# Expert results of a routed layer: six picked rows a token, or two token-ordered sums in DRAM built by adding writes

## The reference

```
scores = sigmoid(xf @ w_router)                      # 1024 tokens, 32 experts
topk_idx = 6 experts of each token, out of 4 groups  # chosen by scores + corr_bias
topk_w = scores at topk_idx
y[token] = sum over its 6 experts e of
    topk_w * ( (silu(h @ gate_w[e]) * (h @ up_w[e])) @ down_w[e] )
y = y + shared expert(h)                             # dense, width 352
x = x + gb * y                                       # gb per sequence and channel
```

## Time and profile before

| | us |
|---|---|
| timed runs, median of 3 (lowest to highest) | 442.95 (440.52 to 444.48) |
| span of the profiled execution, first to last instruction | 442.4 |
| expert stage, first to last tile_hidden (L1800) | 112.2 to 251.7 |
| products of the shared expert for sequence 1 (L664) begin | 256.1 |
| first product of layer 1 (L843 on x_r) begins | 283.6 |
| PE busy / DVE busy / ACT busy / POOL busy | 409.2 / 293.6 / 207.5 / 129.4 |

### The profile page before, as it was taken

The page is one execution under the profiler, slowest core; times in us unless marked ns, Lnnn a source line. Parts: engine busy times, 40 slices in busy tenths (PEclk is TensorE's granted clock), DMA queues, the critical chain, the costliest instruction groups (busy, mean ns, idle before and its releaser), DMA issues. The chain is left out here.

```text
span 442.4 us, 6194 instructions
## 1 busy us (share of the span) xinstructions
PE 409.2 (93%) x1923; PEld 305.7 (69%) x1924; DVE 293.6 (66%) x710; ACT 207.5 (47%) x390; POOL 129.4 (29%) x143
## 2 busy tenths in 40 slices
PE   6996888888999999999998899899999979999997
PEld 6453737445677777777776636787677858798886
DVE  4899986898444444444444465989786998886542
ACT  2598935473222222222222237482796487722430
POOL 1000011003777777777777500601000010010000
PEclk9989788997999999999999969999999998999999
DMA  7986665890333233333239249911500000000001
GB/s 272 418 377 150 150 154 142 305 425 26 100 103 107 98 104 107 95 101 106 101 101 276 74 162 369 331 74 28 185 1 0 1 1 1 1 1 35 12 1 48
DMA packets 24010, 56.89 MB, mean 129 GB/s; under 512 B 4528, under 2 KB 15794, under 8 KB 22996
## 3 DMA queue, kind: packets, MB, share of 16 engines
q1 hardware_dynamic: 18564, 41.80, 28.0%
q0 software_dynamic: 5424, 14.82, 10.2%
HBM read 46.10 MB, written 10.50 MB: 128 GB/s over the span
## 5 line engine op out<-in xcount | busy, mean ns | idle before, releaser
L732 PE MATMUL bank<-arena,tile_mem 128*128 x224 | 75.6, 460 | 0.0
L1406 POOL DMA_INDIRECT tile_mem<-h_dram,gidx x57 | 56.1, 984 | 52.5 <-DVE gidx L1784 35.5
L1394 POOL TENSOR_TENSOR rstd<-ve,mhalf 128x2 f32<-128x2 f32 (+1 forms) x14 | 11.2, 800 | 192.1 <-DVE ve L1533 192.1
L1413 POOL DMA_INDIRECT y_dram<-norm,didx x56 | 55.4, 990 | 22.7 <-issue 13.7
L1800 DVE TENSOR_TENSOR tile_mem<-tile_mem,bank 128x176 f32<-128x176 f32 x56 | 18.9, 338 | 62.3 <-ACT tile_mem L1204 62.3
L748 PE MATMUL bank<-arena,tile_mem 88*128 x224 | 57.9, 380 | 0.8 <-DVE tile_mem L1795 0.8
L748 PEld LDWEIGHTS bank<-arena,tile_mem 88*128 88x128 f32 x224 | 42.4, 189 | 15.8 <-issue 1.0
L843 PE MATMUL bank<-x_r,f_r 128*128 128x512 f32 x192 | 46.6, 403 | 0.8 <-DVE x_r L1980 0.7
L732 PEld LDWEIGHTS bank<-arena,tile_mem 128*128 128x128 f32 x224 | 38.2, 190 | 11.8
L1204 ACT ACTIVATE tile_mem<-bank 128x176 f32<-128x176 f32 x56 | 17.8, 317 | 57.4 <-PE bank L732 57.4
L843 PEld LDWEIGHTS bank<-x_r,f_r 128*128 128x128 f32 x192 | 36.9, 194 | 10.0 <-issue 0.8
(11 more groups left out here) (290 smaller groups left out, 740.7 us busy)
## 6 DMA issues: line engine op xcount, KB each, us to landing
arena<-w_gu SPq DMA_DIRECT2D x3, 2112.0 KB, 12.3
arena<-w_dn SPq DMA_DIRECT2D x4, 1408.0 KB
arena<-w_gu SPq DMA_DIRECT2D x2, 2464.0 KB, 21.1
arena<-y_dram SPq DMA_DIRECT2D x6, 768.0 KB, 9.0
arena<-w_f SPq DMA_DIRECT2D x6, 512.0 KB, 6.9
arena<-wmod SPq DMA_DIRECT2D x3, 512.0 KB, 9.1
arena<-wmod SPq DMA_DIRECT2D x2, 768.0 KB, 10.7
arena<-y_dram SPq DMA_DIRECT2D x4, 384.0 KB, 5.5
```

The lines of the kernel that those rows point to most:

```text
L732: mm = pe.matmul(bank[2 + r % 2][:, 0:2 * M], xgT[r % 2][:, k * P:(k + 1) * P], gu[:, bass.ds(e[k], 2 * M)], start=(k == 0), stop=(k == CT ...
L1406: pool.indirect_dma_start(out=xg[j % 4], out_offset=None, in_=h2_dram, in_offset=bass.IndirectOffsetOnAxis(ap=gidx[:, j:j + 1].bitcast(U32 ...
L1413: pool.indirect_dma_start(out=y_dram, out_offset=bass.IndirectOffsetOnAxis(ap=didx[:, j:j + 1].bitcast(U32), axis=0), in_=yt[j % 4], in_of ...
```

## The change

The experts' results are no longer stored apart and picked up later. Two tensors in DRAM, `sum_dram[0]` and `sum_dram[1]`, have one row a token and 128 rows for empty slots. They start with zeros (and, in the first, with the shared expert's result for sequence 0), and the scatter of tile j adds its 128 rows into the one of number j % 2. The score is multiplied in before: it is gathered together with the token's row, since `h2_dram` now has 32 more columns that hold `scores`, and `tile_hidden` multiplies by the column of the tile's expert, whose number DVE reads from `eoff` once a quad. After the experts, SP loads two rows a token in place of six.

With it go other waits: a gather waits for `tile_hidden` of tile j-4 (it used to wait for `tx`); `copy_y` of tile j waits until the scatter of tile j-2 has landed (it used to be j-4); LAG goes from 6 to 5; the sums of sequence 0 are made by DVE alone, behind `shared_hidden`.

```diff
-LAG = 6
+LAG = 5
...
-    h2_dram = nc.dram_tensor("h2_dram", (B * S, C), F32, kind="Internal").ap()
+    h2_dram = nc.dram_tensor("h2_dram", (B * S, C + E), F32, kind="Internal").ap()
-    y_dram = nc.dram_tensor("y_dram", ((TOPK + 1) * B * S, C), F32, kind="Internal").ap()
+    sum_dram = [nc.dram_tensor(f"sum_dram{i}", (P + B * S, C), F32, kind="Internal").ap() for i in range(2)]
...
@@ SP @@
+            sp_.wait_ge(zeros_ready, 1)
+            for i, blocks in ((0, (0, 1)), (0, (1 + TB, 1 + NT)), (1, (0, 1 + NT))):
+                n = blocks[1] - blocks[0]
+                rows = sum_dram[i].rearrange("(n p) c -> p n c", p=P)[:, blocks[0]:blocks[1], :]
+                sp_.dma_start(rows, zeros.unsqueeze(1).to_broadcast([P, n, C])).then_inc(sums_start, 16)
             sp_.wait_ge(modT_done, 2)
             for e in range(0, DN_LATE, 8):
                 sp_.dma_start(dn[:, e * DNW:(e + 8) * DNW], w_dn[:, e * DNW:(e + 8) * DNW]).then_inc(dn_in, 16)
...
-                sp_.dma_start(h2v[:, b * TB:(b + 1) * TB, :], norm[:, b * TB:(b + 1) * TB, :]).then_inc(h2_out, 16)
+                sp_.dma_start(h2v[:, b * TB:(b + 1) * TB, 0:C], norm[:, b * TB:(b + 1) * TB, :]).then_inc(h2_out, 16)
+                sp_.wait_ge(score_ready, b + 1)
+                sp_.dma_start(h2v[:, b * TB:(b + 1) * TB, C:XR], scores[:, b * TB:(b + 1) * TB, :]).then_inc(h2_out, 16)
             sp_.wait_ge(x1_out, 16 * B)
             for e in range(EARLY, E, 6):
                 sp_.dma_start(gu[:, e * GUW:(e + 6) * GUW], w_gu[:, e * GUW:(e + 6) * GUW]).then_inc(gu_late, 16)
+            sp_.wait_ge(shy_ready, 1)
+            sp_.dma_start(sum_dram[0].rearrange("(n p) c -> p n c", p=P)[:, 1:1 + TB, :], shared_y[:, 0:TB, :]).then_inc(sums_start, 16)
...
+            load_sums(0, 0)
+            load_x1(0)
+            load_sums(0, 1)
             for k in range(0, HT, 4):
                 sp_.dma_start(f2w[:, k:k + 4, :], w_f2[:, k:k + 4, :]).then_inc(f2_in, 16)
             sp_.dma_start(w2w, w_2).then_inc(w2_in, 16)
+            for h in range(2):
+                load_sums(1, h)
+            load_x1(1)
...
@@ PE, after the shared expert's first products @@
-            for t in range(TB):
-                choice_sums(t)
             pe.wait_ge(shhid_ready, 2 * SHT)
             shared_out(1, (2, 3), range(TB))
...
@@ POOL @@
             def gather(j):
 
                 if j >= 4:
-                    pool.wait_ge(tx_done, j - 3)
+                    pool.wait_ge(hid_ready, j - 3)
...
             def scatter(j):
 
                 pool.wait_ge(y_ready, j + 1)
-                pool.indirect_dma_start(out=y_dram, out_offset=bass.IndirectOffsetOnAxis(
-                    ap=didx[:, j:j + 1].bitcast(U32), axis=0), in_=yt[j % 4], in_offset=None)\
+                pool.indirect_dma_start(out=sum_dram[j % 2], out_offset=bass.IndirectOffsetOnAxis(
+                    ap=didx[:, j:j + 1].bitcast(U32), axis=0), in_=yt[j % 4], in_offset=None, compute_op=ALU.add)\
                     .then_inc(y_out[j % 4], 16)
...
             pool.wait_ge(didx_ready, 1)
+            pool.wait_ge(sums_start, 16 * 4)
...
@@ DVE @@
+            dve.wait_ge(sums_start, 16 * 3)
             dve.memset(gsx[:, :, G:], BIG)
...
             def tile_hidden(q, r):
 
+                e = dve.snap(regs[r], min_val=0, max_val=E - 1)
                 dve.wait_ge(sil_ready, 4 * q + (r + 1))
-                tt(hid[r % 2], sil[r % 2], bank[2 + r % 2][:, M:2 * M], ALU.mult).then_inc(hid_ready, 1)
+                stt(hid[r % 2], sil[r % 2], xg[r][:, bass.ds(e + C, 1)], bank[2 + r % 2][:, M:2 * M], ALU.mult, ALU.mult)\
+                    .then_inc(hid_ready, 1)
 
             def copy_y(q, r):
                 dve.wait_ge(dn_done, 4 * q + (r + 1))
-                if not early(q, r, 4):
-                    dve.wait_ge(y_out[r], 16 * q)
+                if not early(q, r, 2):
+                    dve.wait_ge(y_out[(r + 2) % 4], 16 * q if r < 2 else 16 * q + 16)
...
             def quad(q, first=False):
+                dve.load(regs, eoff[0:1, bass.ds(4 * q + 1, 4)])
...
+            def routed_sums(b, h):
+
+                pair = slice(2 * h, 2 * h + 2)
+                v, x = routed[b][0][:, pair, :], X2[:, b * TB + 2 * h:b * TB + 2 * h + 2, :]
+                dve.wait_ge(sums_in[b][h], 32)
+                step(tt(v, v, routed[b][1][:, pair, :], ALU.add))
+                settle()
+                if b:
+                    dve.wait_ge(shy_ready, 2)
+                    step(tt(v, v, shared_y[:, b * TB + 2 * h:b * TB + 2 * h + 2, :], ALU.add))
+                    settle()
+                step(tt(v, v, gb0[:, b, :].unsqueeze(1).to_broadcast([P, 2, C]), ALU.mult))
+                settle()
+                dve.wait_ge(x1_in[b], 16)
+                tt(x, x, v, ALU.add).then_inc(comb_done, 2)
+                dve.wait_ge(comb_done, b * TB + 2 * h + 2)
+                for t in range(b * TB + 2 * h, b * TB + 2 * h + 2):
+                    norm_stats(t, x2)
...
-            half_sums(range(2))
-            shared_hidden(1, range(1, SHT))
-            half_sums(range(2, TB))
-            gated_sums(range(2))
-            gated_sums(range(2, TB))
-            variance(4, x2, (0,), stats_done=True)
-            variance(4, x2, (1,))
+            shared_hidden(1, range(SHT))
+            for h in range(2):
+                routed_sums(0, h)
+                variance(4, x2, (h,), stats_done=True)
```

More of the change, by code:

```diff
@@ L298, in two_layers @@
         yg_w = [m[0] if i < 2 else m for i, m in enumerate(yg_mem)]
-        yg = [tiles(m, TOPK) for m in yg_w]
+        routed = [[tiles(m[:, 0:TB * C], TB) for m in yg_w[2 * b:2 * b + 2]] for b in range(B)]
+        zeros = tile_mem[:, (SHT + 1) * S:(SHT + 1) * S + C]
         rS, iS, aS, a2 = [tiles(m[:, 0:RT * S], RT) for m in yg_w]
@@ L1788, in _ @@
             settle()
-            tt(didx[:, :], didx[:, :], drow, ALU.max).then_inc(didx_ready, 1)
+            ts_(didx[:, :], drow, float(P - B * S), par[:, P_J:P_J + 1], ALU.add, ALU.max).then_inc(didx_ready, 1)
             def copy_h(q, r):
```

161 lines of the change are left out of this document (34 added, 127 removed).

## The result

The changed kernel takes 478.75 us (median of 4 runs, 476.85 to 479.82) against 442.69 (4 runs, 440.52 to 444.48) for the kernel before, a ratio of 1.082 (95% interval 1.078 to 1.086). The prediction said 447.3, with 439 to 458 as its range, so it was wrong.

| | before | after | difference |
|---|---|---|---|
| first tile_hidden | 112.2 | 112.5 | +0.3 |
| first to last tile_hidden | 139.5 | 177.4 | +37.9 |
| last tile_hidden to layer 1's first product | 31.9 | 28.4 | -3.5 |
| from there to the first product of the convolution | 6.2 | 8.3 | +2.1 |
| from there to the end | 152.6 | 151.4 | -1.2 |

The account below looks back on a forecast made before the run. PE was taken to bound the expert stage (busy 137.5 of 140 us), with the hidden chain and POOL close behind. 442.95 + 5.4 (stage) - 3.0 (behind the experts) + 2.0 (clock) = 447.35, say 447.3 us; range 439 to 458.

Parts of the forecast that it names:

- The scatter's issue: POOL's time to issue a scatter in the expert stage: taken as unchanged at 1.00 us when adding, harmless up to 1.03.
- the adding scatter is dearer to issue: Rival, chance 0.20: POOL's issue of the scatter grows; at 1.5 us about 470, at 1.15 us 453.
- The register load: DVE's load once a quad, between copy_y and copy_h: needs 0.49 of 0.62 us of cover, so costs nothing.
- the uncovered case: If DVE's register load could not run under copy_y: 0.3 us for each of 14 quads, 4 us.
- The hidden step: tile_hidden's two additions lengthen PE's step by 0.05 to 0.15 us; 0.11 taken, 2.60 a tile, 6.05 us over 55.
- POOL's lead: Gathers wait for tile_hidden of tile j-4: gather 7 moves from 117.08 to about 120, 2.9 us less lead.
- the second wait: A gather's wait for the shared expert's rows in sum_dram[0]: there at 109, write some 3 us, ending no later.
- The stretch with layer 1's weights: Expert stage while those weights load: a gather's wait of 1.4 us where before it was 2.1, so -0.7.
- The landing and its cover: The adding scatter may land up to 4.2 us after issue, from 2.4 plain, before copy_y on DVE waits; cost 0.
- zeros; routing: Writing 1.8 MB of zeros at the start, some 4 us of queue, and the added score writes in routing: cost 0.
- Behind the experts: From the experts' end to layer 1's start: PE's choice_sums go and DVE adds instead; 3.0 us gained.
- The clock: PE idles before layer 1's products, so its granted clock falls to 0.50 for 6.5 us: 2.0 us lost.

Follow-up runs that it names:

- plain_load_moved: plain_writes with DVE's register load moved from the start of a quad to in front of its fourth tile_hidden; 446.44 us (1.008).
- plain_no_score: plain_writes with the score taken out: tile_hidden multiplies silu and up alone, and DVE loads no registers; 446.32 us (1.005).
- plain_writes: The changed kernel with its scatter writing rows without adding, everything else of the change kept; 459.65 us (1.034).
- no_score_early_gather: plain_no_score with each gather waiting for the transposes of the tile four back, as before the change, instead of its tile_hidden; 447.10 us (1.010).
- plain_held_clock: plain_load_moved with nine more 128 x 128 products on PE behind shared_out, into a bank nobody reads; 445.37 us (1.004).

## Why the prediction was wrong

**The scatter's issue: the step that failed.** "I take the same, for lack of a row that says otherwise, and keep the other as a rival": 1.00 us. It is 1.59. With it POOL has 3.186 us of work a tile, more than PE, and the stage runs at POOL's pace: (3.186 - 2.49) x 55 = 38.3, measured 37.9. That the two agree so closely is partly chance, since at both ends of the stage the steps are not POOL's. The rival *the adding scatter is dearer to issue* had the mechanism, the point from which it decides (1.03), and with its 1.5 a time of 470; with 1.59 its own working gives 478. It got a chance of 0.20 and a range cut at 458, which allows only about 1.2 us an issue. The indication for it was a ratio: the Trainium skill (Collectives: The Full Stack, The bandwidth ceiling) has two reads and a write for a reduction, where a copy has one read, which would make three entries for two. The times agree roughly: 1.56 to 0.97, 1.42 to 0.90 and 1.33 to 0.86 are ratios of 1.61, 1.58 and 1.55. The packets of the queue don't: they treble, from 48 to 144, so the near agreement does not show that entries are what POOL's time goes by. With no row on the price of an operation and a whole engine near its limit, that case deserved more than a fifth.

**The register load.** "Nothing, then" rested on PE's 339 ns and on 0.62 us of cover. DVE's load takes 0.96 to 1.10 in that place, and cost 8.6 us of the stage where POOL did not hide it. The price given for the uncovered case, 4 us, was too small by half, since it kept the 339 ns of a load that begins at number 4q. The floor of some 600 ns in the Trainium skill (DMA: Bandwidth & Descriptors, Latency and other measured facts), which the prediction set aside for the 339, is too high for PE and for the fourth step (0.34), and less than the first step takes (0.98).

**The hidden step.** 0.11 a tile was taken, 2.60; PE's own pace became 2.56 in the first steps of the changed kernel, and 2.585 throughout in plain_load_moved, where it sets the pace. Right within the range, but in the changed kernel it decides nothing: behind POOL's 3.19 it is hidden.

**POOL's lead.** Gather 7 was to move from 117.08 to about 120. It came at 120.34 in plain_no_score, as forecast. In plain_writes it came at 121.24: the first tile_hidden is 0.3 later, and the step behind it takes 2.97 us instead of 2.39. In the changed kernel it came at 122.54, with two adding scatters ahead of it. That the second wait "ends no later" held, but just: the shared rows are issued at 109.06 and land 3.7 later (3 were taken), at 112.8, and tile_hidden of tile 0 ends at 112.9. The two waits end together, and the one for the rows, with the LAG of 5, is enough to take the lead away: in no_score_early_gather, where only these two are left, gather 6 comes at 117.96 instead of 114.09 before.

**The stretch with layer 1's weights.** -0.7 was taken. Measured with plain writes and the load moved, the steps there exceed the pace by 4.8 us, where the kernel before lost 2.6. The sum had only looked at gathers. In plain_load_moved copy_y also waits there for the write of two tiles back, 3.7 us in two waits; the longest landing of its trace is 6.0. This is where the shorter wait distance shows after all.

**The landing and its cover; zeros; routing.** 3.8 against a cover of 4.2, and nothing for the rest: right, the stage starts 0.3 later.

**Behind the experts.** -3.0 was taken, -3.5 measured. **The clock** after PE's idle time: +2.0 taken, +2.1 measured. The mechanism is the one forecast: plain_held_clock fills the idle time, and the clock stays up.

With a scatter of 0.99 and a load of 0.35 the kernel stands where the sum put it: plain_load_moved is at 446.4, the sum said 447.3. That agreement is partly luck. In its trace the term for the weights' stretch is too small by some 3 us, and the clock that stays up behind the last tile, which the sum did not have, gives 2.7 back.

## What to carry to other kernels

Add up each engine's instructions per tile and ask which one has the least room left; a change that makes an instruction of that engine dearer is priced first, by itself, before anything it saves elsewhere is counted. An engine whose idle time is all "issue" is the bound, however long others wait for transfers in the table of waits. Costs in a loop hide behind each other: undo them one at a time and together, since moving the load took 8.6 us off the stage under plain writes and 2.6 beside the adding ones. And compare stages, not only whole times: of 12.5 us between two traces here, 3.0 were the clock in another place.

## What the runs showed of the hardware

- An indirect DMA that adds keeps POOL busy for 1.56 us instead of 0.97 with 128 rows, at every row length from 128 to 512 values, and 1.33 instead of 0.86 with 32 rows. Its landing, from issue, is 3.8 us instead of 2.4 for 128 KB, and up to 7.7 in the changed kernel (a plain one up to 6.2 in the kernel before). In the profiles the queue counts 10800 packets instead of 5424 for 57 gathers and 56 scatters: 48 for a plain transfer, so 144 for an adding one.
- A load of four registers on DVE takes 0.34 to 0.35 us in the fourth step of the loop's body, from number 4q + 4 on, and 0.96 to 1.10 in the first step, from 4q + 1 on. Which of the two differences makes it slow was not tested; PE's, at the head of its loop's body and from 4q on, takes 0.34.
- PE's clock went to its lower level behind the last tile in some traces and not in others, whose waits there differ by tenths of a microsecond. With it the same 24 products took 12.1 to 13.6 us instead of 10.56. What decides it there was not found.
- The mean granted clock differs between executions of one kernel, and the time goes with it: the six runs of plain_load_moved at 0.962 to 0.968 took 445.5 to 446.6 us, the four at 0.947 to 0.953 took 447.1 to 450.9.
